# Keys written into their head's columns by ScalarE and VectorE, and a DMA queue that no longer waits in its middle

## What is computed

```python
def xattn(x, y, Wq, Wkv, Wproj, bproj):        # 16 heads of 64, 128 queries and 128 keys per batch
    q = (x @ Wq).reshape(b, lq, H, DK).transpose(0, 2, 1, 3)
    k, v = split((y @ Wkv).reshape(b, lkv, 2, H, DK))
    atten = softmax(einsum('bhid,bhjd->bhij', q, k) * DK ** -0.5)
    return einsum('bhij,bhjd->bhid', atten, v).reshape(b, lq, H * DK) @ Wproj + bproj

def ffn(tokens):                                # 8 experts, the two best of each token
    probs = softmax(tokens @ gate_w.T)
    top2_w, top2_idx = top_k(probs, 2)
    expert_out = silu(tokens @ expert_w[e].T + expert_b[e])
    return (sum of top2_w * expert_out of the two) @ combine_w.T

x = x + xattn(layernorm(x), ctx_768)
x = x + ffn(layernorm(x))
```

## Time and profile before

| | |
|---|---|
| median of 3 runs | 2218.74 us (2216.15 to 2225.38) |
| profiled execution | 2207.19 us, span of its trace 2204.3 us |
| mean granted TensorE clock | 0.909 of full speed |
| TensorE, matmuls | 77% busy |
| VectorE / ScalarE / GpSimd | 56% / 48% / 42% busy |
| DMA traffic | 303.79 MB, 138 GB/s mean |

### The profile page before, as it was taken

How to read it: one execution, slowest core, us unless ns; L and a number is a source line. 1 busy time by engine, 2 the same in 40 slices (tenths; PEclk the granted TensorE clock), 3 DMA queues, 4 the chain that set the end, 5 groups by cost and what they waited for, 6 DMA issues and landing times.

```text
span 2204.3 us, 39447 instructions
## 1 busy us (share of the span) xinstructions
PE 1689.9 (77%) x11835; PEld 1586.3 (72%) x11835; DVE 1225.8 (56%) x3090; ACT 1062.2 (48%) x2904; POOL 922.7 (42%) x1213
## 2 busy tenths in 40 slices
PE   4578898978777778888777777988777778876565
PEld 4578888877767777877777776877777777865454
DVE  5357777766545556776554455666555556643222
ACT  4356566645444445655444444655444445633232
POOL 3335555544333334655333333554333345534032
PEclk9889999999998989999989899999999999987767
DMA  5343332334444444334444454335454453447785
GB/s 177 123 139 82 88 86 77 82 91 130 140 143 135 136 136 127 94 109 144 145 141 146 135 158 147 94 109 171 145 159 133 141 153 113 137 145 231 237 257 175
DMA packets 219978, 303.79 MB, mean 138 GB/s; under 512 B 24725, under 2 KB 184698, under 8 KB 219258
## 3 DMA queue, kind: packets, MB, share of 16 engines
q1 hardware_dynamic: 207482, 267.71, 40.5%
q0 software_dynamic: 12288, 33.57, 5.0%
HBM read 164.06 MB, written 70.01 MB: 106 GB/s over the span
## 4 chain that ended last, share of the span: by engine, by line
PE 38%; DMA 23%; SPq 14%; issue 10%; DVE 8%; POOL 4%; ACT 3%; another core or an unknown queue 0%; POOLq 0%; DVEq 0%; ACTq 0%
DMA k_s<-qk_s 21%; PE s_ps L483 10%; PE gen_ps L483 10%; PE o_ps L483 8%; PE proj_ps L483 4%; SPq L359 4%; PE qk_ps L483 3%; SPq L413 3%; SPq L414 2%; SPq L416 2%; ACT probs L717 2%; PE pT_ps L521 2%; DVE sums L881 1%; DVE pT_s_lo L832 1%; POOL o_s_lo L1134 1%
## 5 line engine op out<-in xcount | busy, mean ns | idle before, releaser
L690 ACT COPY stage<-o_ps 64x256 f32<-64x256 f32 x512 | 188.3, 368 | 801.8 <-PE o_ps L483 788.7
L483 PE MATMUL s_ps<-k_s,qk_s 128*128 128x256 f32 x1536 | 264.8, 313 | 284.2 <-DMA k_s<-qk_s 269.3
L483 PEld LDWEIGHTS s_ps<-k_s,qk_s 128*128 128x128 f32 x1536 | 221.0, 209 | 312.2 <-DMA k_s<-qk_s 297.5
L874 DVE TENSOR_REDUCE neg_max<-s_ps 128x4 f32<-128x512 f32 x256 | 176.5, 690 | 367.0 <-PE s_ps L483 365.1
L881 DVE TENSOR_REDUCE sums<-probs 128x4 f32<-128x512 f32 x256 | 175.6, 686 | 358.4 <-ACT probs L717 358.4
L1132 POOL CAST o_s_hi<-stage 128x256 fp32r<-128x256 f32 x256 | 103.6, 405 | 628.0 <-ACT stage L690 627.3
L1123 POOL TENSOR_TENSOR probs<-probs,inv_sums 128x512 f32<-128x512 f32 x256 | 266.6, 1042 | 222.6 <-DVE inv_sums L883 222.6
L717 ACT ACTIVATE probs<-s_ps,neg_max 128x128 f32<-128x128 f32 x1024 | 292.9, 369 | 29.3 <-DVE neg_max L874 22.8
L483 PE MATMUL proj_ps<-wproj_s_hi,o_s_hi 128*128 128x256 f32 x512 | 158.8, 310 | 89.3 <-POOL o_s_lo L1134 71.1
L1134 POOL TENSOR_TENSOR o_s_lo<-stage,o_s_hi 128x256 fp32r<-128x256 f32 x256 | 187.8, 734 | 21.1
L1154 POOL DMA_INDIRECT stage<-sorted_y,y_row_of x128 | 126.3, 987 | 146.9 <-issue 64.0
(11 more groups left out here) (169 smaller groups left out, 4854.7 us busy)
## 6 DMA issues: line engine op xcount, KB each, us to landing
w_block<-expert_table SPq DMA_DIRECT2D x163, 512.0 KB
k_s<-qk_s SPq DMA_DIRECT2D x512, 128.0 KB
stage<-sorted_x SPq DMA_DIRECT2D x163, 128.0 KB
sorted_y<-stage SPq DMA_DIRECT2D x163, 128.0 KB
x_raw<-in_x SPq DMA_DIRECT2D x32, 256.0 KB
c_raw<-in_ctxT SPq DMA_DIRECT2D x32, 256.0 KB
stage<-in_x SPq DMA_DIRECT2D x32, 256.0 KB
x_kept<-x SPq DMA_DIRECT2D x32, 256.0 KB
```

The costliest lines, as they stand in the source:

```text
L483: mm = pe.matmul(out_ap, l, r, start=start and n == 0, stop=stop and n == len(terms) - 1, skip_group_check=skip)
L690: last = act.copy(to, of)
L874: dve.tensor_reduce(neg_max[p % 2][:, :], s_ps[:, :].rearrange("p (k n) -> p k n", k=4), AX_X, ALU.max, negate=True).then_inc(max_done, 1)
```

## The change

Three things are done.

1. `spread_keys`, its two DMAs per slot and the semaphores `k_in` are gone. `qk_s` becomes `q_s` (queries only), and `qk` on ScalarE and on VectorE writes the keys straight into the diagonal blocks of `k_s`. Each of the two engines so has three instructions (128x256, 64x256, 64x256) where it had one (128x512). `k_s` has its head and part dimensions exchanged. `scores` waits for `qk_lo`.
2. ScalarE's `attended` moves from the end of slot u, for `u-1`, to the place behind `exps` in slot u + 1.
3. `load_block` is cut in two. `load_rows` (the block's rows of x) runs two slots ahead, `load_expert` (its weights, which hold the wait for `expert`) one slot ahead, and `store_block` one slot later and behind both.

```diff
-            def spread_keys(j, p):
-                n = j * HEAD_PAIRS + p
-                sp.wait_ge(qk_lo, n + 1)
-                wait(sp, s_made, n - 1)
...
-                for h in range(2):
-                    rows = slice(h * HALF, (h + 1) * HALF)
-                    sp.dma_start(k_s[p % 2][rows, :, h, :].bitcast(F32),
-                                 qk_s[p % 2][rows, :, N2:].bitcast(F32)).then_inc(k_in[p % 2], 16)
...
-            def load_block(c, b, n):
+            def load_rows(c, b, n):
                 r = n % RING
                 if b == 0:
                     sp.wait_ge(blocks_done, c + 1)
                     for half in range(2):
                         wait(sp, scattered[half], 64 * ((plan.ends[c] + 1 - half) // 2))
+                    sp.wait_ge(cleared, 16 * E * (c + 1))
+                if n == 0:
+                    sp.wait_ge(dump_cleared, 16)
+                wait(sp, made["turn_block"], n - RING + 1)
+                row = sp.value_load(blocks[b:b + 1, c, 0:1], min_val=0, max_val=ROWS - P)
+                sp.dma_start(x_block[r], sorted_x[bass.ds(row, P), :]).then_inc(x_block_in[r], 16)
+
+            def load_expert(c, b, n):
...
                 wait(sp, made["expert"], n - RING + 1)
                 e = sp.value_load(blocks[b:b + 1, c, 1:2], min_val=0, max_val=E)
                 sp.dma_start(w_block[r][:, :, :].bitcast(F32).rearrange("p a n -> p (a n)"),
...
-                if s - 2 in plan.turn:
-                    store_block(*plan.turn[s - 2])
                 if s + 2 in plan.turn:
-                    load_block(*plan.turn[s + 2])
+                    load_rows(*plan.turn[s + 2])
+                if s + 1 in plan.turn:
+                    load_expert(*plan.turn[s + 1])
+                if s - 3 in plan.turn:
+                    store_block(*plan.turn[s - 3])
...
             def scores(j, p):
-                pe.wait_ge(k_in[p % 2], 32 * ((j * HEAD_PAIRS + p) // 2 + 1))
+                pe.wait_ge(qk_lo, j * HEAD_PAIRS + p + 1)
...
             def qk(j, p):                      # ScalarE
                 n = j * HEAD_PAIRS + p
                 wait(act, s_made, n - 1)
-                split_hi(qk_made, n + 1, [(qk_s[p % 2][:, 0, :], qk_ps[:, :])], qk_hi)
...
+                split_hi(qk_made, n + 1, [
+                    (q_s[p % 2][:, 0, :], qk_ps[:, 0:N2]), (kh[0:HALF, 0, 0, :], qk_ps[0:HALF, N2:]),
+                    (kh[HALF:P, 1, 0, :], qk_ps[HALF:P, N2:])], qk_hi)
...
                 if now:
                     exps(i, u)
+                if u < 2 and before:
+                    attended(i - 1, 6 + u)
+                if u >= 2 and now:
+                    attended(i, u - 2)
...
-                if u == 0 and before:
-                    attended(i - 1, 7)
-                if u > 0 and now:
-                    attended(i, u - 1)
...
             def qk(j, p):                      # VectorE
                 split_lo(qk_hi, j * HEAD_PAIRS + p + 1, [
-                    (qk_s[p % 2][:, 1, :], qk_ps[:, :], qk_s[p % 2][:, 0, :])], qk_lo)
+                    (q[:, 1, :], qk_ps[:, 0:N2], q[:, 0, :]),
+                    (k[0:HALF, 0, 1, :], qk_ps[0:HALF, N2:], k[0:HALF, 0, 0, :]),
+                    (k[HALF:P, 1, 1, :], qk_ps[HALF:P, N2:], k[HALF:P, 1, 0, :])], qk_lo)
```

More of the change, by code:

```diff
@@ L169, in xattn_moe_kernel @@
         v_s = hilo("v_s", [P, 2, D])
-        qk_s = [sb(f"qk_s{b}", [P, 2, 2 * N2], F32R) for b in range(2)]
+        q_s = [sb(f"q_s{b}", [P, 2, N2], F32R) for b in range(2)]
         k_s = [sb(f"k_s{b}", [P, 2, 2, N2], F32R) for b in range(2)]
@@ L260, in xattn_moe_kernel @@
         x1_saved = sem("x1_saved")
-        k_in = [sem(f"k_in{b}") for b in range(2)]
         scattered = [sem(f"scattered{b}") for b in range(2)]
@@ L348, in load_ctx @@
                 sp.dma_start(c_raw[:, :, :], ctxT[j].rearrange("p (a n) -> p a n", a=2)).then_inc(c_in, 16)
-            def spread_keys(j, p):
-                n = j * HEAD_PAIRS + p
-                sp.wait_ge(qk_lo, n + 1)
-                wait(sp, s_made, n - 1)
-                if n < 2:
-                    sp.wait_ge(zeroed, 2)
-                for h in range(2):
-                    rows = slice(h * HALF, (h + 1) * HALF)
-                    sp.dma_start(k_s[p % 2][rows, :, h, :].bitcast(F32),
-                                 qk_s[p % 2][rows, :, N2:].bitcast(F32)).then_inc(k_in[p % 2], 16)
             def clear_after(c):
@@ L399, in load_block @@
                         wait(sp, scattered[half], 64 * ((plan.ends[c] + 1 - half) // 2))
+                    sp.wait_ge(cleared, 16 * E * (c + 1))
[5 more added lines that the diff above has]
+            def load_expert(c, b, n):
+                r = n % RING
+                if b == 0:
+                    sp.wait_ge(blocks_done, c + 1)
                 if n < RING:
@@ L403, in load_block @@
                     sp.wait_ge(table_stored[r], 16 * count)
-                if b == 0:
-                    sp.wait_ge(cleared, 16 * E * (c + 1))
                 if n == 0:
                     sp.wait_ge(bias_stored, 96)
[L408 to L411, removed]
                 wait(sp, made["expert"], n - RING + 1)
@@ L434, in _ @@
             for s, i, u in slots():
[L435 to L438, removed]
                 if u == 3 and exists(i):
@@ L512, in scores @@
                     mm = products(s_ps[:, t * N2:(t + 1) * N2].rearrange("p (h n) -> p h n", h=2), three(
-                        (0, 1), (0, 1), lambda part: qk_s[p % 2][:, part, t * P:(t + 1) * P],
-                        lambda part: k_s[p % 2][:, part, :, t * P:(t + 1) * P]))
+                        (0, 1), (0, 1), lambda part: q_s[p % 2][:, part, t * P:(t + 1) * P],
+                        lambda part: k_s[p % 2][:, :, part, t * P:(t + 1) * P]))
                 mm.then_inc(s_made, 1)
@@ L723, in qk @@
                 wait(act, s_made, n - 1)
-                split_hi(qk_made, n + 1, [(qk_s[p % 2][:, 0, :], qk_ps[:, :])], qk_hi)
+                kh = k_s[p % 2]
+                if n < 2:
+                    act.wait_ge(zeroed, 2)
+                split_hi(qk_made, n + 1, [
+                    (q_s[p % 2][:, 0, :], qk_ps[:, 0:N2]), (kh[0:HALF, 0, 0, :], qk_ps[0:HALF, N2:]),
+                    (kh[HALF:P, 1, 0, :], qk_ps[HALF:P, N2:])], qk_hi)
             def pT(j, p):
@@ L885, in qk @@
             def qk(j, p):
+                q, k = q_s[p % 2], k_s[p % 2]
                 split_lo(qk_hi, j * HEAD_PAIRS + p + 1, [
-                    (qk_s[p % 2][:, 1, :], qk_ps[:, :], qk_s[p % 2][:, 0, :])], qk_lo)
+                    (q[:, 1, :], qk_ps[:, 0:N2], q[:, 0, :]),
+                    (k[0:HALF, 0, 1, :], qk_ps[0:HALF, N2:], k[0:HALF, 0, 0, :]),
+                    (k[HALF:P, 1, 1, :], qk_ps[HALF:P, N2:], k[HALF:P, 1, 0, :])], qk_lo)
             def pT(j, p):
```

## The result

The changed kernel takes 1950.85 us (median of four runs, 1948.61 to 1953.8), the kernel before 2217.44 us (four runs, 2208.04 to 2225.38): a ratio of 0.88 [0.8763, 0.8837]. The forecast was 1922 us with a range of 1860 to 2030, so the time lies 29 us (1.5%) above the point. In spans the miss is larger: 1909 us were added up and 1948.4 measured, 39 us more.

The account below looks back on a forecast made before the run. The kernel was taken as bound by keys' transfers queued behind SyncE's wait for `expert`, at TensorE's lower clock. From 2204.3 us: expert slots -283, plain +28, first 16 -32, tail -8, giving 1909, scaled to 1922 us; range 1860 to 2030.

Parts of the forecast that it names:

- The transfers and the queue: In expert slots, the 5.75 us between TensorE's end and `scores` go, and the lower clock with them; 283 us less.
- The move of `attended`: A loss in plain slots: ScalarE's copies now stand behind `exps` in a loop through TensorE, 0.75 us of it.
- The ring: Loop in each slot: `exps`, copies, GpSimd's split, `project`, `scores`, `row_max`, next `exps`; no slot under 5.55 us.
- the expert slots' 6.8: Us taken per slot for 83 of the 122 slots with an expert block, those with final sums; 6.6 for 39.
- Three instructions for one: ScalarE's high parts cost about 1.03 us instead of 0.47, VectorE's low parts 1.2; small-job slots take 5.86 us.
- the rival of half-price pieces: ScalarE's and VectorE's three pieces and the copies overlap fully, about 0.3 us less in 239 slots; 1850 us, chance 0.10.
- the term of the plain slots: The 117 attention slots without an expert block take 735 us for 707, so 28 more.
- 117 x 6.09 = 712: Plain slots at the mean of eight undisturbed ones, 6.09 us each against 5.51; 712 us for 645.
- the clock falls: Rival: idle time ahead of `project` in every slot keeps TensorE at its lower clock; 2990 us, chance 0.02.
- the 23 us kept of the 62.6: Plain slots' excess over undisturbed ones: 40 us of waits for keys go, 23 stay for VectorE's listing and final sums.
- The smaller terms: First 16 slots take 99 us for 131.5, so 32 less; the tail, with no keys, 8 less.
- The rivals of the weights and of the queue: Block weights limit expert slots, 2007 us, chance 0.15; SyncE's queue still holds TensorE by late weights or rows, 2148 us, 0.03.

Follow-up runs that it names:

- run 7: The changed kernel with TensorE doing the four transposes of each `turn_x` job four times over, the last result being used: 1914.97 us, ratio 0.8706.
- run 3: The kernel before with keys written directly, and with the old queue and `attended` in its old place: 1857.97 us, ratio 0.8446.
- run 4: The kernel before with the new order in SyncE's queue alone, keys still going by two transfers in each slot: 1884.33 us, ratio 0.8534.
- run 2: The changed kernel with the old queue, `load_block` in one piece and the stores as before: 1952.96 us, ratio 0.8842.
- run 1: The changed kernel with `attended` back in its old place at the end of ScalarE's slot: 1875.74 us, ratio 0.8491.
- run 5: The kernel before with the move of `attended` alone, old keys and old queue: 2230.54 us, ratio 1.0138.

## Why the prediction was right in the whole, and wrong by 29 us

**The transfers and the queue: right, but two cures for one illness.** The expert slots came to 833.1 us against 822 forecast, at a clock of 0.97 to 1.00; 7 of the 11 us missing are in the first stage, and run 7 gives them back. What the forecast put under one heading, runs 3 and 4 take apart: each of the two edits alone brings the gain (1858 and 1884 us). The queue adds nothing to direct keys (run 2 against the changed kernel). Direct keys add 9 us to the queue (run 1 against run 4, same chip): they gain 35 in the first 16 slots and cost 20 in the plain and expert slots. The keys were late because they were queued behind SyncE's wait for `expert`. Let the wait be for a block one slot older, whose `expert` is done when SyncE comes to it, and a transfer of 128 KB is early enough; take the transfer away and the wait matters to nobody. The forecast never gave the parts their own prices, and so did not say that one of them could be left out.

**The move of `attended`: a loss, rightly signed, but more than plain slots.** The ring was right: 5.53 us at u = 0, forecast 5.55. Run 1 prices the move at 75 us by the medians, 78 by the spans (57 in plain slots, 29 in expert slots, less 8 that it gains, nearly all in the first 16), once the keys are direct, run 5 at 25 us with the old keys and queue. The forecast priced it in plain slots only, and took the expert slots' 6.8 as given.

**Three instructions for one: right.** The casts and copies took what was forecast. This is VectorE's timeline in the kernel after; the whole low part runs from 258.70 to 259.89:

```profile
258.70 0.42 DVE L827 TENSOR_TENSOR q_s<-qk_ps,q_s 128x256 fp32r<-128x256 f32 x1 [0.22 <-ACT k_s L680]
259.04 0.85 DVE L827 TENSOR_TENSOR k_s<-qk_ps,k_s 64x256 fp32r<-64x256 f32 x2
259.92 0.26 DVE L915 TENSOR_REDUCE logits<-gen_ps 128x8 f32<-128x16 f32 x2
```

The pair takes 0.85 us, twice 0.42, and the next instruction starts 0.03 after its end, whereas `k_s` began 0.08 ahead of the end of `q_s`. That makes 1.2 in the queue. By the rule of the Trainium skill (VectorE: DVE Perf Modes, "Two Vector instructions with no wait between them"), that an instruction whose output starts in another quarter of the partitions is held for all before it, the upper half had to wait; the trace agrees, and the rival of half-price pieces falls with it. The kinds of slot came out one by one: u = 1 at 5.87 (forecast 5.86), u = 2 at 6.25 (6.3), u = 3 at 7.11 where the clock held (7.1), u = 5 and 7 at 6.15 and 6.06 (6.0 and 6.15); expert slots 5.80 without a small job (5.8) and 6.41 with one (6.4). The expert slot at u = 5 was forecast too low, at no more than 7.1 without final sums, and took 7.40 to 7.55 there.

**The step that failed** is the term of the plain slots, 735 us, which measured 769.7. Its part "117 x 6.09 = 712" holds for clean slots, as run 7's pair shows at 48.7 us. Two things were wrong beside it.

The first is the lower clock, which the term left out. I had dismissed it with one row: TensorE stood 2.36 us ahead of `project` and the clock stayed at 1.00. That row is one of fifteen, and the trace of the kernel before holds the others. These are the u = 3 slots of pairs 3 and 4 there, first as windows and then by the first matmuls of `project`:

```profile
222.90:231.20 8.30, 0.66 (x1) 1.14 (x4) 0.82 0.58 155
268.60:275.70 7.10, 0.68 (x1) 1.14 (x4) 1.00 0.58 158
```

```profile
228.26 0.58 PE L483 MATMUL proj_ps<-wproj_s_hi,o_s_hi 128*128 128x256 f32 x1 [2.36 <-POOL o_s_lo L1134]
228.64 0.42 PE L483 MATMUL proj_ps<-wproj_s_lo,o_s_hi 128*128 128x256 f32 x1
228.85 0.41 PE L483 MATMUL proj_ps<-wproj_s_hi,o_s_lo 128*128 128x256 f32 x1
...
273.98 0.39 PE L483 MATMUL proj_ps<-wproj_s_hi,o_s_hi 128*128 128x256 f32 x1 [2.36 <-POOL o_s_lo L1134]
274.20 0.28 PE L483 MATMUL proj_ps<-wproj_s_lo,o_s_hi 128*128 128x256 f32 x1
274.32 0.28 PE L483 MATMUL proj_ps<-wproj_s_hi,o_s_lo 128*128 128x256 f32 x1
```

The idle time is the same, and in the first slot the matmuls start 0.21 us apart, in the second 0.12: those are the two levels of the clock, 1.2 and 2.4 GHz. Of the 15 plain u = 3 slots of the kernel before, 6 fell to the lower level at some point and took 7.53 to 8.36 us; the other 9 took 7.10 to 7.12. In the kernel after 13 of 15 fell (7.25 to 8.34 us), and so did the five of the first stage with expert blocks, after some 2.05 us of idle time; the slot behind each was longer too, by up to 1 us. Run 7 changes only how much TensorE has to do at u = 3. None of its 15 fell, and 19 us of the 35 missing in the plain slots came back, with the clock at 0.98. The Trainium skill (TensorE: Matmul & The Clock Gate, "What's actually happening") has it that the lower clock is the default and activity releases the higher one. That agrees with run 7, in which more work of TensorE made these slots shorter. So the rival "the clock falls" came true in part: as a cost of some tens of us, not as the collapse to 2990 that I had priced. There was no case between none of it and all of it.

The second is the 23 us kept of the 62.6 beyond the clean slots. In run 7, where u = 3 and 4 are clean, 38 us are left. The four slots in which lists are made take 9.9 to 10.0 us, 3.8 above what the forecast has for their kind and 15 in all; in the kernel before they took 10.0 to 10.2. What did go is mainly a wait for keys behind each list: the four slots at u = 1 that held it took 9.3 to 11.0 us before and 5.9 to 6.6 after. Together, 19 and 15, the two parts make up the 35.

**What was luck.** The sum of the spans was 39 us short. The point was only 29 short because the forecast carried the kernel before's ratio of median to profiled run, 1.0052 or 10 us, over to the kernel after, whose profiled run (1950.14) lies at its median. And the sum would have been 47 short without the first 16 slots, which came out 8 us below their term.

**The smaller terms.** The first 16 slots took 91.1 us, 8 less than forecast, for they ran at clock 1.00 (5.7 a slot, where 6.2 was taken). The tail took 224.2, forecast 222; over the eleven traces it went from 209 to 230 us, and what sets it was not tried. The rivals of the weights and of the queue did not occur: TensorE's waits for `w_block` come to 14.3 us over the whole span of the kernel after, and run 4 moved 203 GB/s in expert slots.

**What stays open**: why the clock fell in some u = 3 slots and not in others with the same 2.36 us of idle time; what makes the tail 10 us or more shorter in the kernels of one chip than in those of another; and the shorter first 16 slots of run 5.

## What to carry to other kernels

When a small transfer is late, look first at what stands ahead of it in its queue: moving one load, and the stores, a slot later, so that the load's wait is over when the queue reaches it (run 4), gave 325 us, where that and replacing 512 transfers with work on two busy engines gave 333 (run 1), and it keeps those engines free for the slots in which they are the bound. Before an operation on an in-order engine is moved forward, add up the loop that it is moved into; 0.75 us of copies inside the ring cost this kernel some 75 us. Once slots are bound by such loops, ask of each in-order engine what it does just ahead of the instruction that the loop waits for: one scatter of 1.07 us, which waited for nothing of that moment, was worth 56 us. Give a lower clock a price per idle stretch in the forecast, not only as all or nothing, and look at all slots of a kind, not at one: 6 of 15 had shown it before the change. And when a total moves, see first that it moved in the stages which the edit touches.

## What the runs showed of the hardware that was not expected

- The same idle stretch of TensorE, 2.36 us ahead of `project` in plain u = 3 slots, brought the lower clock in 6 of 15 slots of the kernel before and in 13 of 15 of the kernel after. With 1.05 us (run 7) none of 15 fell. It is not in itself a safe or an unsafe amount.
- Matmuls of no use (three further rounds of four transposes per job) made the plain slots 19 us and the expert slots 7 us shorter in sum.
- ScalarE does not overlap two successive copies into different halves of the partitions either: in the chain of the kernel after the second `k_s` starts only when the first has ended and takes its full 0.38, where `q_s` and the first `k_s` add 0.27 and 0.26 to it.
- The DMA engines carried 203 GB/s at a share of 0.69 beside expert slots of 6.7 us (run 4), with key transfers among them that were in time.
